# A macaron block (feed-forward, linear attention, feed-forward) on one core: the feed-forward's sum of inner units in SBUF instead of PSUM, a ring of four banks, and another order in the prologue

## The reference

```python
x = x + 0.5 * ffn(layernorm(x))
x = x + attn(layernorm(x))
x = x + 0.5 * ffn(layernorm(x))          # the same weights as the first

def ffn(x):                              # M = 64, INNER = 16
    s = x @ Win + bin_                   # (b, t, 64)
    h = relu(s[..., None] * W1 + b1)     # (b, t, 64, 16), elementwise
    g = einsum('btmh,mh->btm', h, W2) + b2
    return g @ Wout + bout

def attn(x):                             # 16 heads of 32
    q, k, v = split(x @ w_attn);  q, k = elu(q) + 1, elu(k) + 1
    # causal linear attention: S += k v^T, z += k, y = q S / (q z + 1e-6)
    return y @ w_proj
```

## Time and profile before

| | us |
|---|---|
| median of 3 runs | 2348.46 (2348.26 to 2348.95) |
| the profiled execution | 2347.02 |
| its span, first to last instruction | 2345.3 |
| TensorE matmuls busy | 2262.0 (96%) |
| TensorE weight loads busy | 1763.3 (75%) |
| VectorE busy | 1908.0 (81%) |
| ScalarE busy | 1431.0 (61%) |
| GpSimd busy | 840.1 (36%) |
| TensorE's mean granted clock | 0.985 |

### The profile page before, as it was taken

How to read it: one execution, slowest core, us unless ns; L and a number is a source line. 1 busy time by engine, 2 the same in 40 slices (tenths; PEclk the granted TensorE clock), 3 DMA queues, 4 the chain that set the end, 5 groups by cost and what they waited for, 6 DMA issues and landing times.

```text
span 2345.3 us, 75312 instructions
## 1 busy us (share of the span) xinstructions
PE 2262.0 (96%) x32834; PEld 1763.3 (75%) x32834; DVE 1908.0 (81%) x3363; ACT 1431.0 (61%) x2285; POOL 840.1 (36%) x864
## 2 busy tenths in 40 slices
PE   2999999999999999999999999999999999999995
PEld 1777777777777777777777777777777777777774
DVE  5879888889888888888889888888888888887766
ACT  5656666556656556657556657555657555656554
POOL 4424333334343334333333343333333333333322
PEclk6999999999999999999999999999999999999997
DMA  6001111111111111102111102111101111101111
GB/s 176 21 13 45 42 35 57 56 54 40 47 31 57 56 56 38 57 21 56 56 56 38 56 21 57 56 56 38 56 21 56 56 56 38 56 23 36 38 38 38
DMA packets 49660, 111.57 MB, mean 48 GB/s; under 512 B 8241, under 2 KB 10289, under 8 KB 45234
## 3 DMA queue, kind: packets, MB, share of 16 engines
q1 hardware_dynamic: 49330, 106.74, 15.7%
HBM read 72.12 MB, written 34.60 MB: 46 GB/s over the span
## 4 chain that ended last, share of the span: by engine, by line
PE 93%; DVE 3%; issue 1%; ACT 1%; SPq 1%; DMA 1%; POOL 0%; DVEq 0%; POOLq 0%; ACTq 0%
PE bank L1131 39%; PE att L1131 23%; PE att L1237 6%; PE att L1158 6%; PE att L1262 5%; PE att L1179 3%; PE bank L1188 3%; PE att L1253 2%; PE bank L1225 2%; PE bank L1179 1%; PE bank L1205 1%; PE bank L1273 1%; DVE acc_psum L792 1%; PE att L1225 1%; DVE st L754 0%
## 5 line engine op out<-in xcount | busy, mean ns | idle before, releaser
L493 ACT ACTIVATE xhat<-res,nmr,rstd 128x512 f32<-128x512 f32 x384 | 297.5, 806 | 327.0 <-DVE nmr L762 292.1
L510 ACT ACTIVATE ffr<-ffs,b1c,w1c 128x512 f32<-128x512 f32 (+2 forms) x560 | 432.8, 792 | 22.9 <-DVE acc_psum L792 18.7
L397 POOL TENSOR_SCALAR_AFFINE_SELECT A<-A 128x512 f32<-128x512 f32 x256 | 157.9, 635 | 734.1 <-ACT A L468 734.1
L792 DVE SCALAR_TENSOR_TENSOR acc_psum<-ffr,w2c,acc_psum 128x512 f32<-128x512 f32 (+2 forms) x525 | 382.4, 728 | 38.3 <-ACT ffr L510 16.9
L386 POOL TENSOR_TENSOR res<-res,hbout 128x512 f32<-128x512 f32 x256 | 324.3, 1290 | 3.4 <-ACT xhat L493 3.4
L393 POOL TENSOR_TENSOR A<-qT,A 128x512 f32<-128x512 f32 x128 | 218.1, 1704 | 291.6 <-DVE qT L821 154.7
L754 DVE BATCH_NORM_STATS2 st<-res 128x6 f32<-128x512 f32 x384 | 260.3, 678 | 17.1 <-DMA res<-in_L_attn_x_dram 12.5
L1131 PE MATMUL att<-xh,wa_h 128*128 128x512 f32 x644 | 258.8, 402 | 2.1 <-DVE xl L771 1.5
L1131 PE MATMUL att<-xl,wa_h 128*128 128x512 f32 x644 | 255.3, 396 | 0.0
L1131 PE MATMUL att<-xh,wa_l 128*128 128x512 f32 x644 | 255.0, 396 | 0.0
L1131 PE MATMUL bank<-wa_h,xh 128*128 128x512 f32 x512 | 217.9, 426 | 0.0
(11 more groups left out here) (120 smaller groups left out, 5113.6 us busy)
## 6 DMA issues: line engine op xcount, KB each, us to landing
xf<-scratch SPq DMA_DIRECT2D x128, 256.0 KB, 4.4
res<-in_L_attn_x_dram SPq DMA_DIRECT2D x31, 1024.0 KB, 5.7
out_dram<-res SPq DMA_DIRECT2D x31, 1024.0 KB, 4.4
scratch<-rden SPq DMA_DIRECT2D x128, 8.0 KB, 1.7
res<-in_L_attn_x_dram SPq DMA_DIRECT2D x4, 256.0 KB, 3.6
kT<-in_L_attn_w_attn_dram SPq DMA_DIRECT2D x1, 1024.0 KB, 6.2
qT<-in_L_attn_w_attn_dram SPq DMA_DIRECT2D x1, 1024.0 KB, 9.1
v<-in_L_attn_w_attn_dram SPq DMA_DIRECT2D x1, 1024.0 KB, 11.3
```

The lines of the kernel that those rows point to most:

```text
L397: eng.affine_select(out=A[:, h, :, :], in_=A[:, h, :, :], compare_op=ALU.is_ge, fill=0.0, base=0, pattern=[[0, 4], [1, P]], channel_multip ...
L493: eng.activation(xhat[t % 2][:, :], res[b % SLOTS][:, t, :], ACT.Identity, bias=nmr[:, n, b % 2, t:t + 1], scale=rstd[:, n, b % 2, t:t + 1 ...
L510: eng.activation(ffr[i % 2][p, w], ffs[p, w], ACT.Relu, bias=b1c[p, i:i + 1], scale=w1c[p, i:i + 1]).then_inc(s_hr, 1)
L792: eng.scalar_tensor_tensor(psum[p, w], r[p, w], w2c[p, i:i + 1], psum[p, w], ALU.mult, ALU.add).then_inc(s_hm, 1)
```

## The change

`acc` is an SBUF buffer of 128 x 512 fp32, and takes the place of acc_psum in `hidden` and `sums` of VectorE and in `sums` of ScalarE. The bank that this leaves becomes the first of a ring of four, and `give` deals the products out anew with it. In the prologue load(1) stands ahead of the ten small loads, and SP waits for the end of ff_in(-2) ahead of wa_st[0]. GpSimd does weights_lo(0) ahead of rstds(L2, 0), and waits for shift(L2, 0) before weights_lo(2).

```diff
--- before.py
+++ after.py
@@ -100,9 +100,9 @@
         att = ctx.enter_context(nc.psum_tensor("att", [P, 4, 512], F32))
 
         ffh, ffl = (y[0][:, :, :].rearrange("p g n -> p (g n)") for y in (yh, yl))
-        psum = ctx.enter_context(nc.psum_tensor("acc_psum", [P, BLK], F32))
-        rest = [ctx.enter_context(nc.psum_tensor(f"bank{i}", [P, 512], F32)) for i in range(5, 8)]
-        bank = {**{h: att[:, h, :] for h in range(4)}, **{5 + i: t[:, :] for i, t in enumerate(rest)}}
+        acc = sb("acc", [P, BLK])
+        rest = [ctx.enter_context(nc.psum_tensor(f"bank{i}", [P, 512], F32)) for i in range(4, 8)]
+        bank = {**{h: att[:, h, :] for h in range(4)}, **{4 + i: t[:, :] for i, t in enumerate(rest)}}
 
 
         s_ld = [sem(f"s_ld{i}") for i in range(SLOTS)]
@@ -183,7 +183,7 @@
 
 
 
-        ATT, RING = (0, 1, 2, 3), (5, 6, 7)
+        ATT, RING = (0, 1, 2, 3), (4, 5, 6, 7)
 
         def emptied(kind, b, i):
 
@@ -306,13 +306,14 @@
                 eng.dma_start(wo_st[M * h:M * h + M, :], Wout).then_inc(s_wo, 16)
             wa_v = w_attn.rearrange("(k p) n -> p k n", p=P)
             eng.dma_start(wa_st[1][:, :, :], wa_v[:, :, C:2 * C]).then_inc(s_wa[1], 16)
+            load(1)
             for dst, src in ((w1c, W1), (b1c, b1), (w2c, W2)):
                 for h in range(2):
                     eng.dma_start(dst[M * h:M * h + M, :], src).then_inc(s_small, 16)
             for h in range(2):
                 eng.dma_start(binc[M * h:M * h + M, :], bin_.rearrange("(m a) -> m a", a=1)).then_inc(s_small, 16)
                 eng.dma_start(b2c[M * h:M * h + M, :], b2.rearrange("(m a) -> m a", a=1)).then_inc(s_small, 16)
-            load(1)
+            e.wait_ge(s_fi, 1)
             eng.dma_start(wa_st[0][:, :, :], wa_v[:, :, 0:C]).then_inc(s_wa[0], 16)
             eng.dma_start(wa_st[2][:, :, :], wa_v[:, :, 2 * C:3 * C]).then_inc(s_wa[2], 16)
             load(2)
@@ -404,8 +405,9 @@
                 bias(1, 0, t)
             weights_lo(1)
             rstds(L1, 1)
+            weights_lo(0)
             rstds(L2, 0)
-            weights_lo(0)
+            e.wait_ge(s_nmr[L2], 1)
             weights_lo(2)
             weights_lo("p")
 
@@ -517,7 +519,7 @@
                     e.wait_ge(s_po, 4 * min(j, NB - 1) + 3)
                 elif j == -1:
                     e.wait_ge(s_fo[1], TILES)
-                copy(ffh[p, columns(j)], psum[p, columns(j)], s_uh)
+                copy(ffh[p, columns(j)], acc[p, columns(j)], s_uh)
 
             def channels(b, t):
                 e.wait_ge(s_xT, 4 * b + t + 1)
@@ -786,17 +788,17 @@
                 e.wait_ge(s_hr, hid(j, i))
                 if i == 0:
                     e.wait_ge(s_small, ALL_SMALL)
-                    eng.tensor_scalar(psum[p, w], r[p, w], w2c[p, 0:1], b2c[p, 0:1], ALU.mult, ALU.add).then_inc(s_hm, 1)
+                    eng.tensor_scalar(acc[p, w], r[p, w], w2c[p, 0:1], b2c[p, 0:1], ALU.mult, ALU.add).then_inc(s_hm, 1)
                     return
                 e.wait_ge(s_hm, hid(j, i) - 1)
-                eng.scalar_tensor_tensor(psum[p, w], r[p, w], w2c[p, i:i + 1], psum[p, w],
+                eng.scalar_tensor_tensor(acc[p, w], r[p, w], w2c[p, i:i + 1], acc[p, w],
                                          ALU.mult, ALU.add).then_inc(s_hm, 1)
 
             def sums(j):
                 p = halves(j)
                 e.wait_ge(s_uh, j + 3)
                 w = columns(j)
-                lo_part(ffl[p, w], psum[p, w], ffh[p, w], s_ul)
+                lo_part(ffl[p, w], acc[p, w], ffh[p, w], s_ul)
 
             def ff_out(half, b, t):
                 r = res[b % SLOTS]
```

## The result

The changed kernel takes 2486.8 us (median of 4 runs, 2485.0 to 2489.3), the one before 2348.4 beside it: a ratio of 1.0594, 95% interval 1.0578 to 1.0611. It is slower by 5.9%, about 139 us, inside the range of the prediction; the point of 2532 was 45 us too high.

A forecast was written before the change was run, and what follows sets the result against it. TensorE, busy 96% of the span, was taken to bound the kernel, with about 0.24 us of slack for VectorE's ysplit. 2347.0 + 189 (passes) - 4.6 (prologue) = 2531.4, about 2532 as median; 8 in 10 for 2420 to 2640.

The forecast's parts named there:

- The mechanism: Passes: hiddens with two SBUF inputs and GpSimd's masks and bias additions lock each other out, delaying TensorE; +189 us.
- Rival A: Passes: the lock does not bind hidden, so only the prologue counts; 2343.9 us, chance 0.06.
- D: Prologue: its gain fails through a late load or a lock elsewhere, passes lose about nothing; 2348 us, chance 0.02.
- C: Passes: besides the lock, a hidden is as slow as the scan, 1.22 instead of 0.75 us; 2711 us, chance 0.07.
- The other signs: Profile after: L792's mean about 1.2 us, L386's about 1.8, TensorE's waits on VectorE's yl up to about 130.
- tile 0: Each pass: hiddens and bias additions take turns, ysplit ends 2.3 us late, TensorE loses 2.2 us.
- tile 1: Each pass: a late hidden, ScalarE's order and hidden 9 push back GpSimd's masks before attend; TensorE loses 1.4 us.
- tile 2: Each pass: GpSimd's masks meet one hidden; 0.2 to 0.6 us, taken as 0.4 us.
- tile 3: Each pass: hiddens 13 to 15 wait for masks and bias additions, the last ysplit delays outer(3); 2.0 us.
- rival B: Passes: the lock binds only partly, as VectorE gets in first more often; 1 to 3 us a pass, 2375 to 2440, chance 0.10.
- The clock: Passes: TensorE keeps its full clock, since single gaps stay near 2 us.
- The prologue: Before the passes: GpSimd's order starts xhat 4.3 us earlier, the loads give 0.3; -4.6 us, or -2.3 if the clock rises no earlier.

The follow-up runs named there:

- Experiment 4: Changed kernel with seven of a pass's eight GpSimd bias additions put ahead of its first mask: 2367.7 us, 1.0098 of the kernel before.
- experiment 5: Kernel before with only the sum moved to SBUF, and the first of two ffr buffers put in the freed PSUM bank: 2400.1 us, 1.0240.
- experiment 1: Kernel before with only the prologue's edits (loads' order with SP's wait, GpSimd's order), sum in PSUM, ring of three: 2338.8 us, 0.9970.
- experiment 3: Kernel before with the sum in SBUF and the ring of four, prologue as before: 2494.1 us, 1.0640.
- Experiment 9: Kernel before with load(1) ahead of the small loads and GpSimd's new order, without SP's wait, sum in PSUM: 2337.5 us, 0.9965.

## Why the prediction was right, and where it was off

**The mechanism held.** The lock read from two rows of a four-column instruction carried over to large ones (435 of 128x512), wherever they meet GpSimd's masks or bias additions; TensorE, full in the passes, bore next to nothing; its two large stalls, 60.7 and 30.8 us, are at places named, `scores(1)` and `outer(3)`. Experiment 4 takes most of the neighbours away and most of the loss goes, experiment 5 takes the second SBUF input away and the hold goes. One step had no ground: that hidden 0, with one large input, would be locked out as well. No row of before showed that; it came true, and why is not shown beyond the three cases of experiment 5. Rival A (no lock) and D are out; so is C: a hidden with both inputs in SBUF and no GpSimd beside it takes 0.75 us (1.59 for two in the rows above), as taken. The Trainium skill (Vector Engine (DVE) Microarchitecture Reference, "Points that are easy to get wrong") gives such an instruction half throughput; these rows disagree, and the measurement decides.

**The size was off: 4.5 us a pass instead of 6.0.** The term that was mis-sized is the price of one meeting. I put a waiting pair at 0.75 + 1.25 = 2.0 us. Four bias additions with hiddens between take 6.36 us, and each later one about 1.72: a pair takes 1.7 us, so about 0.3 us of the two rows lies outside the time for which they shut each other out. The other signs are smaller in the same way: 1.12 us for the sum (forecast about 1.2), 1.60 for the bias addition (1.8), 100 us of waits for ysplit (130). By tile, against before:

| | forecast us | measured us |
|---|---|---|
| tile 0 | 2.2 | 2.2 to 2.4 (11.37 between the scores, 8.97 and 9.22 before) |
| tile 1 | 1.4 | 0.65, and 1.5 with the half clock |
| tile 2 | 0.4 | 0.0 (6.67 us, 6.65 before) |
| tile 3 | 2.0 | 1.1 to 1.2 |

The times between scores take two values each before, by turns from pass to pass. Tile 0 agrees by luck, by two errors that cancel: I let hidden 3 in ahead of the first addition, but the addition had started at 555.62 and the hidden at 555.67, so there was one more meeting, each cheaper. In tile 3 each hidden takes 1.16 to 1.18 us instead of up to 1.4.

In tile 1 the path was wrong as well. I had TensorE wait at `attend` for GpSimd's masks, pushed back by ScalarE's order, and held that the one bias addition behind them ends before `ynorm`. A pass at full clock, TensorE and then VectorE:

```profile
1833.86 1.17 PE L1239 MATMUL att<-qT,kT 32*128 32x128 f32 x32 [0.60 <-DVE yl L773]
...
1837.38 1.10 PE L1264 MATMUL att<-A,v 128*32 128x128 f32 x32
...
1841.37 1.17 PE L1239 MATMUL att<-qT,kT 32*128 32x128 f32 x32 [0.59 <-DVE yl L773]
```

```profile
1836.43 2.89 DVE L794 SCALAR_TENSOR_TENSOR acc<-ffr,w2c,acc 128x512 f32<-128x512 f32 x2
1839.24 0.69 DVE L852 TENSOR_TENSOR att<-att,xf 128x512 f32<-128x512 f32 x1
```

`attend` comes 3.52 us behind the scores, 3.53 before: the masks cost nothing here, and `attend` waits for them for 0.6 us in the whole trace. Hidden 9 and 10, beside that bias addition, take 2.89 us and hold back ynorm, ysplit and the scores of tile 2. The rival B ("partly bound", up to 2440) is not what happened: the meetings shown do cost, and are cheaper.

**The clock.** I forecast full clock in the passes because single gaps would stay near 2 us, having seen a gap of that size (2.5 us ahead of an `attend`) before without a fall. That step failed: 16 passes have 3.4 us of half clock behind such a gap. It costs 14 us, and hides some of the wait behind it: in tile 1 VectorE's lateness (0.65) and the slower clock (1.5) take each other's place.

**The prologue.** Forecast -4.6 us, of it 4.3 by GpSimd's order. shift(L2, 0) does take 0.16 us, hidden 0 is locked out until 26.2, and the first projection starts at 53.02 instead of 56.33: -3.3, in a run whose block 0 landed 1.5 us later. But the scores of pass 0 come at 101.47 instead of 99.68. In between, hiddens of j = -1 hold up GpSimd's zsum and themselves, and TensorE waits for it in `den`:

```profile
87.46 0.42 PE L1207 MATMUL bank<-A,heads_of 128*32 128x128 f32 x8 [1.21 <-POOL A L394]
89.92 0.66 PE L1207 MATMUL bank<-A,heads_of 128*32 128x128 f32 x8 [2.03 <-POOL A L394]
```

I had given these hiddens 1 us; from the first projection to the scores of pass 0 it is 48.45 us, 43.35 before and 43.42 in experiment 1, so they cost 5. By the medians the changed kernel is still 0.46% under experiment 3, some 11 us. In the profiled executions it is 5.4 us, none of it in the prologue (the scores of pass 0 begin at 101.12 in experiment 3, at 101.47 in the changed kernel): it is fewer passes with a half-clock stretch (16 instead of 23, at 0.9 us), for which I have no cause. The other half stays open.

## The version that beats both

Experiment 9: the sum in its PSUM bank, the ring of three, load(1) ahead of the small loads, and GpSimd's new order. 2337.5 us, 8.0 below before and by the ratios some 147 below the change. Experiment 1, with SP's wait, is as fast within the noise.

## What to carry to other kernels

Before a buffer that VectorE reads moves from PSUM to SBUF, count the SBUF inputs of each instruction that reads it and lay GpSimd's timeline beside it: the second SBUF input makes the two engines take turns. Look too at single-input instructions that would then go from SBUF to SBUF, as hidden 0 does here. If the other engine is in order and full, every microsecond of that lateness counts at the next hand-over, while the share of busy time hardly moves (81 to 83%). Where the buffer must move, first move GpSimd's work into the stretch where VectorE has no such instruction: here that took back 116 of 139 us.

## What the runs showed that I had not expected

- Two instructions that shut each other out overlap in their rows: a pair takes 1.70 us, not the 2.0 of its rows alone. The Trainium skill (SBUF — State Buffer, "Who interferes with whom") calls the shared port pair an exclusive lock, and says that a VectorE instruction with two SBUF inputs contends with a GpSimd instruction that reads SBUF. The rows agree, and the turns overlap by about 0.3 us a pair.
- TensorE's clock falls to half for 3.4 us behind some idle stretches of about 2 us and not behind others of the same length.
- The stall inside the first ff_in that no semaphore ends (4.55 us before) took 1.30 us with one 1 MB load put earlier in the queue and no load held back. What it waits for, the trace doesn't show.
